# The first attention sequence of a 32-sequence transformer kernel in an order of its own

## The reference

```python
q = l2norm(q)
k = l2norm(k)
dots = jnp.einsum('bhid,bhjd->bhij', q, k) * QK_SCALE
dots = jnp.einsum('hg,bgij->bhij', W_pre_th, dots)
...
dots = jnp.where(causal[None, None], mask_value, dots)
top = jax.lax.top_k(dots, TOPK)[0]
vk = top[..., -1:]
dots = jnp.where(dots < vk, mask_value, dots)
attn = jax.nn.softmax(dots, axis=-1)
attn = jnp.einsum('hg,bgij->bhij', W_post_th, attn)
out = jnp.einsum('bhij,bhjd->bhid', attn, v)
...
out = out * jax.nn.sigmoid(gates)
return out @ Wo
```

## Time and profile before

| | us |
|---|---|
| three runs, median | 3628.78 |
| three runs, lowest and highest | 3628.4 and 3636.17 |
| the profiled execution | 3634.36 |
| its span, first to last instruction | 3633.1 |
| busy in the span: PE, DVE, ACT, POOL | 3390.1, 3437.1, 3092.9, 1745.4 |

### The profile page before, as it was taken

How to read it: one execution, slowest core, us unless ns; L and a number is a source line. 1 busy time by engine, 2 the same in 40 slices (tenths; PEclk the granted TensorE clock), 3 DMA queues, 4 the chain that set the end, 5 groups by cost and what they waited for, 6 DMA issues and landing times.

```text
span 3633.1 us, 78764 instructions
## 1 busy us (share of the span) xinstructions
PE 3390.1 (93%) x19287; PEld 2527.5 (70%) x19287; DVE 3437.1 (95%) x18664; ACT 3092.9 (85%) x10837; POOL 1745.4 (48%) x3670
## 2 busy tenths in 40 slices
PE   4999999986999999999999999999999999999987
PEld 2888888863666666676676666666666666666665
DVE  7999999936999999999999999999999999999993
ACT  6888888856898899989899898998998998898863
POOL 0000000014666666666666666666666666666663
PEclk9999999997999999999999999999999999999998
DMA  3000000002222222222222222222222222222210
GB/s 132 11 14 13 13 12 13 10 13 85 73 71 78 82 66 65 65 66 66 66 65 66 74 71 70 74 73 79 79 66 65 65 66 65 67 65 66 73 55 4
DMA packets 254141, 210.74 MB, mean 58 GB/s; under 512 B 78000, under 2 KB 234736, under 8 KB 252912
## 3 DMA queue, kind: packets, MB, share of 16 engines
q1 hardware_dynamic: 253680, 205.70, 18.1%
HBM read 93.97 MB, written 111.67 MB: 57 GB/s over the span
## 4 chain that ended last, share of the span: by engine, by line
PE 66%; ACT 17%; DVE 11%; issue 4%; POOL 2%; DMA 0%; SPq 0%; DVEq 0%; ACTq 0%; POOLq 0%
PE bank L378 10%; PE bank L221 8%; PE bank L1434 6%; PE bank L1422 5%; PE bank L1407 5%; PE bank L1465 3%; PE bank L469 3%; PE bank L195 3%; ACT SN L1618 3%; PE bank L1499 3%; DVE W L1826 3%; PE bank L1479 3%; PE bank L1438 3%; PE bank L346 3%; ACT sq L496 2%
## 5 line engine op out<-in xcount | busy, mean ns | idle before, releaser
L1826 DVE MATCH_REPLACE8 W<-last,W 128x130 f32<-128x130 f32 (+18 forms) x3456 | 871.9, 259 | 0.0
L1848 DVE MAX8 last<-W 128x8 f32<-128x130 f32 (+18 forms) x3456 | 762.9, 262 | 0.0
L1933 POOL TENSOR_SCALAR posts<-post,share 128x128 f32<-128x128 f32 x1024 | 366.7, 378 | 284.0 <-DVE share L1755 279.1
L1602 ACT ACTIVATE T<-T,peak 128x260 f32<-128x260 f32 (+15 forms) x1024 | 410.9, 409 | 3.5 <-POOL T L1984 2.4
L1618 ACT ACTIVATE SN<-bank,rq 128x260 f32<-128x260 f32 (+1 forms) x1024 | 357.9, 424 | 61.3 <-PE bank L1407 60.8
L1422 PE MATMUL bank<-T,pre 128*128 128x40 f32 (+15 forms) x1024 | 365.3, 439 | 14.4 <-ACT T L1626 10.1
L1434 PE MATMUL bank<-posts,T 128*128 128x128 f32 (+7 forms) x2048 | 311.7, 289 | 68.9 <-POOL posts L1933 60.6
L1984 POOL TENSOR_TENSOR T<-T,below 128x520 f32<-128x520 f32 (+12 forms) x416 | 360.3, 882 | 20.0 <-DVE below L1857 4.6
L1434 PEld LDWEIGHTS bank<-posts,T 128*128 128x128 f32 (+7 forms) x2048 | 249.0, 174 | 165.3 <-POOL posts L1933 88.9
L938 DVE TENSOR_TENSOR_SCAN hs<-dA,dx 128x256 f32<-128x256 f32 x512 | 349.9, 684 | 2.9 <-ACT dA L800 1.9
L1949 POOL TENSOR_TENSOR T<-T,w_mask 128x32 f32<-128x32 f32 x512 | 141.1, 278 | 412.6 <-ACT T L1626 410.2
(11 more groups left out here) (242 smaller groups left out, 9572.3 us busy)
## 6 DMA issues: line engine op xcount, KB each, us to landing
scores_by_token<-SN SPq DMA_DIRECT2D x64, 520.0 KB, 2.6
scores_by_token<-SN SPq DMA_DIRECT2D x64, 396.0 KB, 3.1
scores_by_token<-SN SPq DMA_DIRECT2D x32, 780.0 KB, 3.3
scores_by_token<-SN SPq DMA_DIRECT2D x32, 264.0 KB, 2.6
scores_by_token<-SN SPq DMA_DIRECT2D x32, 260.0 KB, 2.0
T<-scores_by_token SPq DMA_DIRECT2D x32, 244.0 KB, 3.0
T<-scores_by_token SPq DMA_DIRECT2D x32, 228.0 KB, 3.2
T<-scores_by_token SPq DMA_DIRECT2D x32, 212.0 KB, 3.8
```

The lines of the kernel that those rows point to most:

```text
L1602: act.activation(one, one, ACT.Exp, bias=peak[k % 2][:, j:j + 1], accum_out=total[k % 4][:, j:j + 1]).then_inc(e_made, 1)
L1826: dve.match_replace(both[:, s, at:to], best[n], both[:, s, at:to], LOWEST).then_inc(ranked, 1)
L1848: dve.max(best[n], both[:, s, at:to]).then_inc(ranked, 1)
L1933: pool.tensor_scalar(posts[(4 * k + j) % NP][:], post[:], share[k % 2][:, j:j + 1], 1.0, ALU.mult, ALU.mult).then_inc(posts_made, 1)
```

## The change

1. **The first sequence ahead of the tables.** For b = 0 the sixteen pieces of blk 1 are made first, then the six of blk 0, into a ring of six banks instead of three. Even pieces are copied by ACT (`first_keep`), odd ones by DVE (11 groups of `TENSOR_SCALAR`, semaphore `s_halved`). Blk 0's scores are kept in `T8[1]`, which is empty then. SP stages blk 1, then blk 0, and regroups pairs of blk 1 and blk 0 in turn (`FIRST`). All 16 premixes, copies and masks of b = 0 stand ahead of the first period, K pieces and squares of b = 1 before them, drops of quad 0 after the sixth mask. DVE clears `V2` and `T8[1]`, POOL no longer does. `tails()` comes in period 1 at beat 12, exponentials of quad 0 at beat 24, `q_clip` of b = 1 at beat 70.
2. **Narrow maxima ahead.** The maximum of quad i + 1's narrow pair (`largest`) stands inside quad i's wide steps, before the second halving; `top` has three buffers. Only quad 0's stays at the start.
3. **Marks by row.** The mark of row n waits for its own row's last `MAX8` only.
4. **Root sooner.** `PE_SPREAD2` 114 to 111, `POOL_ROOT2` 118 to 116.
5. **The last sequence** loads its exp table ahead of `nd.act_square`.

The diff, cut to its core:

```diff
+FIRST_SCORES = [(blk, piece) for blk in (1, 0) for piece in range(len(S_PIECES[blk]))]
...
+    FIRST = [(blk, k) for k in range(QUADS) for blk in (1, 0)]
...
-    top, last8 = room.sbs("top", [P, 4, 8], 2), room.sbs("last8", [P, 4, 8], 2)
+    top, last8 = room.sbs("top", [P, 4, 8], 3), room.sbs("last8", [P, 4, 8], 2)
...
+    FIRST_SN = (T8[1][:, 0:HEADS * W_LO].rearrange("p (h n) -> p h n", h=HEADS), SN)
+    FIRST_BANK = [*FRONT, *ATB, BACK[1]]
...
+    TAILS, FIRST_EXP, FIRST_CLIP = 12, 24, 70
...
-    PE_SPREAD2 = 114
+    PE_SPREAD2 = 111
...
-    POOL_ROOT2 = 118
+    POOL_ROOT2 = 116
...
             if seq(f):
...
+                else:
+                    stage(0, 1)
+                    stage(0, 0)
+                    for blk, k in FIRST:
+                        regroup(0, blk, (k,))
...
+        for blk, piece in FIRST_SCORES[::2]:
+            score(0, blk, piece)
+        for f in range(2):
+            front.k_piece(pe, 1, 0, f)
+        for blk, k in FIRST:
+            premix(0, blk, k)
...
+        first_keep()
+        for f in range(2):
+            front.k_square(act, 1, 0, f)
+        for blk, k in FIRST:
+            t_keep(0, blk, k)
+            if (blk, k) in ((0, 4), FIRST[-1]):
+                peaks(0, int(k > 4))
...
+                    if b == SEQS - 1:
+                        table(EXP_LN)
                     nd.act_square(act, b)
...
+        def largest(b, i):
...
+            dve.wait_ge(masked, masked_at(b, low))
+            dve.tensor_reduce(top[k % 3][:, 2:4, 0], side_by_side(b, low), AXIS.X, ALU.max).then_inc(ranked, 1)
...
                 if done == 3:
+                    if j0 == 0 and i + 1 < QUADS and QUAD[i + 1][2] not in WIDE:
+                        largest(b, i + 1)
+                        yield
...
-                dve.wait_ge(found_wide, 2 * ((QUADS + 1) * b + i + j0 // 2 + 1))
...
                 for n, (j, s) in enumerate(rows):
+                    dve.wait_ge(found_wide, 2 * ((QUADS + 1) * b + i + j0 // 2) + n + 1)
...
+        for n, (blk, piece) in enumerate(FIRST_SCORES):
+            if n % 2:
+                dve.wait_ge(s_made, n + 1)
...
+                    last = dve.tensor_scalar(FIRST_SN[blk][:, h, 0:w], FIRST_BANK[n % 6][:, j * w:(j + 1) * w], rq[:, c:c + 1], None, ALU.mult)
+                last.then_inc(s_halved, 1)
+        dve.memset(V2[:], 0.0)
+        for sent in staged[0]:
+            dve.wait_ge(sent, 16)
+        dve.memset(T8[1][:], 0.0).then_inc(blanked, 1)
...
+        for blk, k in FIRST:
+            hide(0, blk, k)
+            if (blk, k) == (0, 2):
+                turn_over(0, 0)
+                drop(0, 0)
+                front.k_clip(pool, 1, 0)
```

More of the change, by code:

```diff
@@ L1147, in attention_phase, with mixed_as, masked_at @@
     PREMIX = [list(range(HALF)), [g for i in range(QUADS) for g in (30 - 2 * i, 31 - 2 * i)]]
-    PAIR_AT = {g: (blk * HALF + k) // 2 for blk in range(2) for k, g in enumerate(PREMIX[blk])}
+    FIRST = [(blk, k) for k in range(QUADS) for blk in (1, 0)]
+    def mixed_as(b, blk, k):
+        return FIRST.index((blk, k)) if b == 0 else HALF * b + QUADS * blk + k
+    def masked_at(b, g):
+        blk = int(g >= HALF)
+        return mixed_as(b, blk, PREMIX[blk].index(g) // 2) + 1
     SN = room.sb("SN", [P, HEADS, KEYS])
@@ L1210, in rank_steps @@
     def rank_steps(i):
-        n = sum(17 for g in QUAD[i] if g in WIDE) + (QUAD[i][2] not in WIDE) + 2 * len(CUT[i])
+        n = sum(17 for g in QUAD[i] if g in WIDE) + (i == 0) + (i + 1 < QUADS and QUAD[i + 1][2] not in WIDE) + 2 * len(CUT[i])
         for g in QUAD[i]:
@@ L1327, in stage, with regroup @@
             for n, (lo, hi, pieces) in enumerate(STAGES[blk]):
-                sp.wait_ge(s_kept, S_ALL * b + S_BEFORE[blk] + pieces)
-                sp.dma_start(by_token[blk][:, lo:hi, 0:w], SN[:, lo:hi, 0:w]).then_inc(staged[blk][n], 16)
-        def regroup(b, blk):
+                if b:
+                    sp.wait_ge(s_kept, S_ALL * b + S_BEFORE[blk] + pieces)
+                else:
+                    kept = FIRST_SCORES.index((blk, 0)) + pieces
+                    sp.wait_ge(s_kept, kept)
+                    sp.wait_ge(s_halved, kept // 2)
+                by_head = SN if b else FIRST_SN[blk]
+                sp.dma_start(by_token[blk][:, lo:hi, 0:w], by_head[:, lo:hi, 0:w]).then_inc(staged[blk][n], 16)
+        def regroup(b, blk, pairs=range(HALF // 2)):
             if b == 1 and blk == 0:
-                sp.wait_ge(zeroed, 2)
+                sp.wait_ge(blanked, 1)
             if b >= 2 and blk == 0:
@@ L1338, in regroup @@
                 sp.wait_ge(sent, 16 * (b + 1))
-            for k in range(HALF // 2):
+            for k in pairs:
                 g = PREMIX[blk][2 * k]
@@ L1357, in sync @@
             if seq(f):
-                stage(f, 0)
-                regroup(f, 0)
-                stage(f, 1)
-                regroup(f, 1)
+                if f:
+                    for blk in range(2):
+                        stage(f, blk)
+                        regroup(f, blk)
+                else:
+                    stage(0, 1)
+                    stage(0, 0)
+                    for blk, k in FIRST:
+                        regroup(0, blk, (k,))
             if f == 0:
@@ L1393, in score @@
         def score(b, blk, piece):
-            n = S_BEFORE[blk] + piece
+            n = S_BEFORE[blk] + piece if b else FIRST_SCORES.index((blk, piece))
             if n == 0:
@@ L1406, in score @@
                     rows = slice(half * DH, (half + 1) * DH)
-                    last = pe.matmul(FRONT[(n + half) % 3][:, j * w:(j + 1) * w], qT[rows, even // 2, blk * P:(blk + 1) * P],
+                    last = pe.matmul((FRONT[(n + half) % 3] if b else FIRST_BANK[(n + half) % 6])[:, j * w:(j + 1) * w], qT[rows, even // 2, blk * P:(blk + 1) * P],
                                      kT[rows, even // 2, 0:w], start=True, stop=True)
@@ L1598, in exps @@
             else:
-                act.wait_ge(masked, HALF * b + PAIR_AT[QUAD[i][2 * pair]] + 1)
+                act.wait_ge(masked, masked_at(b, QUAD[i][2 * pair]))
             for j in (2 * pair, 2 * pair + 1):
@@ L1619, in s_keep, with first_keep @@
             last.then_inc(s_kept, 1)
+        def first_keep():
+            act.wait_ge(q_root.stepped, Root.STEPS)
+            for n, (blk, piece) in enumerate(FIRST_SCORES):
+                if n % 2 == 0:
+                    act.wait_ge(s_made, n + 1)
+                    w = (W_LO, W_HI)[blk]
+                    for j, h in enumerate(S_PIECES[blk][piece]):
+                        c = blk * HEADS + h
+                        last = act.activation(FIRST_SN[blk][:, h, 0:w], FIRST_BANK[n % 6][:, j * w:(j + 1) * w], ACT.Copy, scale=rq[:, c:c + 1])
+                    last.then_inc(s_kept, 2)
         def t_keep(b, blk, k):
             pair = pair_scores(b, PREMIX[blk][2 * k])
-            if (b, blk, k) == (0, 0, 0):
-                tails()
-            act.wait_ge(premixed, 2 * PAIRS * b + PAIRS * blk + k + 1)
+            act.wait_ge(premixed, mixed_as(b, blk, k) + 1)
             act.activation(pair, MIX[:, 0:pair.shape[-1]], ACT.Copy).then_inc(t_kept, 1)
@@ L1810, in wide @@
             rows = [(j, side(QUAD[i][j])) for j in (j0, j0 + 1)]
-            best = [top[k % 2][:, j, :] for j, _ in rows]
+            best = [top[k % 3][:, j, :] for j, _ in rows]
             for n, (j, s) in enumerate(rows):
@@ L1867, in rank @@
                 dve.wait_ge(peaked, k - 1)
-            if low not in WIDE:
-                dve.wait_ge(masked, HALF * b + PAIR_AT[low] + 1)
-                dve.tensor_reduce(top[k % 2][:, 2:4, 0], side_by_side(b, low), AXIS.X, ALU.max).then_inc(ranked, 1)
-                count += 1
+            if i == 0:
+                largest(b, i)
                 yield
```

77 lines of the change are left out of this document (47 added, 30 removed).

## The result

| | before | changed |
|---|---|---|
| median of 8 runs | 3628.35 us | 3642.37 us |
| lowest and highest | 3619.96 and 3636.17 | 3640.71 and 3643.46 |
| profiled execution, its span | 3634.36, 3633.1 | 3642.25, 3640.9 |
| ratio, 95% interval | | 1.0040 (1.0031 to 1.0048) |

The change costs 14 us. Forecast were 3620.5, faster, with a range of 3601 to 3632; the time lies above it.

What follows compares the result with a forecast made beforehand. The PE and ACT loop was taken as the bound, DVE nearly tied. From a median of 3628.8, −11.3 + 0.9 − 0.6 − 0.6 + 3.9 − 0.6 = −8.3 gave 3620.5 us, range 3601 to 3632.

Steps and rivals of the forecast that it cites:

- The start: Prologue: ranking of the first sequence starts at about 835.4 instead of 846.70, 11.3 us sooner (bounds 9 and 17).
- The fill on DVE: Prologue, DVE clearing T8[1]: 3.83 to 5.3 us, hidden behind transfers and first mix, 1.6 us of cover at worst.
- What comes back: First period: q_clip six beats later and PE's Q turn cost +1.5 us (0 to 2.6), net +0.9.
- Rival C: Prologue's gain swallowed: DVE memset, shared DMA queue or second sequence's premix late by 3 to 7 us; 3623.5 to 3627.5; chance 0.24.
- Maxima ahead and marks by row: Each period: 0.55 us less DVE work, only 0.02 on the path; −0.6 us in 30 periods, −0.6 in the last.
- Rival A: DVE is the bound: 17.6 us of DVE work and 6.6 of x_d waits come off; 3594, or 3601 without waits; chance 0.20.
- DVE's wait at the first halving: DVE at L1803 in each period: wait for POOL's mask grows from 0.36 to about 0.9 us.
- The waits for x_d: DVE's six waits on PE, 6.6 us in all, vanish with the root sooner, but gain nothing.
- Root sooner: PE's spread of nd's root, each period: a gap of 0.13 us (0 to 0.30), +3.9 us in all (0 to 9).
- rival B: Load of nd_rs after mix-back 4: spread waits longer, 30 us per us of gap, slower from 0.65 (3636 and more); chance 0.08.
- The table at the end: Last sequence: ACT's exp table load ahead of the squares no longer delays the root, −0.6 us.

Runs made afterwards that it cites:

- e7: Changed kernel with the root put back and the second sequence's whole K chain placed between the first sequence's sixteen mixes; 3619.88 us, 0.9980 of before.
- e11: Changed kernel, root put back, K steps among mixes from the fourth, tails ahead of mixes, quad 0-2 steps sooner, q_clip at beat 64; 3610.97 us, 0.9954 of before.
- e4: Kernel before with only the maxima ahead, marks by row and last table sooner (parts 2, 3, 5); 3623.41 us, 0.9996 of before.
- e2: Kernel before with only the nd root sooner (PE at beat 111, POOL at 116); 3631.15 us, 1.0013 of before.
- e12: Kernel before with root sooner, maxima ahead, marks by row and last table sooner, but the old first sequence; 3635.59 us, 1.0019 of before.
- e9: Kernel before with only the first sequence's new order (part 1), DVE's waits at the marks in their old order; 3639.30 us, 1.0027 of before.
- e3: Kernel before with only the first sequence's new order (part 1), one extra DVE wait per quad, mark waits exchanged; 3651.89 us, 1.0071 of before.
- e5: Kernel before with only the first sequence's new order (part 1), no extra quad wait, but DVE's two mark waits exchanged; 3656.50 us, 1.0076 of before.

## Why the prediction was wrong

**The start: right in its sum, with luck in its terms.** Forecast 835.4, measured 833.7. The scores with their copies took 8.3 us and not 13.5 (44 products at 810.33 and 6.13 us in the chain, then 2.19 of copies): back to back at the low clock four products took 0.86 us (810.90 to 811.76) and not the 1.24 of the single row that I had scaled, and the clock rose to its full level at about 813.5. The copies ended 6.5 us sooner than in my sum, but the last staging transfer landed 7.6 us behind them, at 826.26, and not 3.4. These two errors offset each other in good part. The fill on DVE took 3.79 us, inside my bounds of 3.83 and 5.3 but for 0.04, and ended 2.5 us ahead of the first maximum, which waited for POOL.

**What comes back: the step that failed.** I wrote that "q_clip for the second sequence moves from beat 64 to 70", priced the wait for quad 3's drops, gave 1.3 to "PE's own Q turn", and took +1.5. It was +19.6. I had treated the first period as one that shifts as a whole with its start. I followed the mixes in the order tables, and not what they were put ahead of: K's root, scaling and second product of the next sequence on three engines. In the trace of before that chain was in plain view (ACT at 846.23, half a microsecond ahead of the first ranking), and from q_clip to the second start are 48.0 us in before (884.44 to 932.46) and 50.0 in the changed kernel (889.13 to 939.09). Had I carried q_clip through the new order, the second start would have come out no sooner than before. e7 and e11 show the cause by moving it. I had also priced PE's clock for the scores alone: that the mixes would run at its low level, some 10 us on PE, stands in no term. Rival C named the outcome, and its sign came true (a start at 833.7 with a second start no sooner than before), but of its causes, the fill on DVE, the DMA queue and the premix of the second sequence, none was this chain, and its price of 3 to 7 us was too small.

**Maxima ahead and marks by row: right.** 0.5 us less of DVE work per period, of which next to nothing shows: e4 is at 0.9996. Rival A is out, and with it, for this kernel, the advice of the Trainium skill that sided with it ("Perfetto Trace Analysis", section "Identifying the Most-Contended Engine": optimise the engine with the highest occupancy first): DVE was 98.9% busy, and less work for it bought nothing that the times can tell. DVE's wait at the first halving grew by 0.24 us and not by 0.5; `share` now waits too, 31 times for 13.0 us in all. The waits for x_d went, as forecast.

**Root sooner: right mechanism, a third of its size.** The gap was forecast at 0.13, with 0.30 as its bound. Alone it is 0.09 by the period (e2). In the whole change it is 0.44 by the timeline and 0.5 by the period. I had kept POOL's times of before for a kernel whose DVE work I had moved. POOL's two marks together took 0.42 us longer, and its last drop and root came that much later against the mix-back. The decision point of rival B was 0.41 us of gap, and its sign, a period of 85.1 or more, came true. By its mechanism and place B was right, without the price of the first period that came on top. Its chance of 0.08 was too low: I had let no cost of one part depend on another part.

The Trainium skill has the rule that would have warned me ("SBUF — State Buffer", section "Who interferes with whom"): a DVE instruction with two inputs in SBUF contends with a GpSimd instruction that reads SBUF. The halvings have two such inputs, and the trace agrees in its direction: 706 ns against 842. Which of the two is held back depends, by the same page, on which was first. But the halvings ran beside these marks in the kernel before as well, for 463 ns of a mark on the mean and 537 in the changed one, so the overlap as such does not explain it; where in a mark it falls may. No run here moved the two against each other by hand, so that this is the cause of the 0.14 us is argued from the rows, not shown; that the gap needs the moved maxima and marks is shown (e2 against e12).

**The table at the end: right.** Forecast −0.6. PE's wait ahead of the last spread fell from 2.55 to 1.92 us (kernel before, then changed):

```profile
3629.52 1.22 PE L134 MATMUL bank<-w_ident,nd_rs 128*128 128x128 f32 x4 [2.55 <-POOL nd_rs L90]
```

```profile
3637.37 1.23 PE L135 MATMUL bank<-w_ident,nd_rs 128*128 128x128 f32 x4 [1.92 <-POOL nd_rs L91]
```

For the rest of the 4.2 us gained at the end the profiles show another clock. The granted clock was 0.53 and 0.50 in the kernel before while the last mix-back and the attention ran, and stayed full in the changed one. Whether the change has a part in that is open: from the last start to the end were 140.4 to 145.4 us in the kernels with parts 2 and 3, and 142.1 to 146.1 in those without. The windows, before and then changed (the clock is the third number from the end):

```profile
3580.00:3585.00 5.00, 3.47 (x14) 2.50 (x14) 0.00 (x0) 0.67 (x3) 1.86 (x5) 0.53 0.01 3
3585.00:3590.00 5.00, 4.05 (x30) 2.91 (x32) 0.00 (x0) 1.50 (x5) 0.11 (x1) 0.50 0.00 0
```

```profile
3592.00:3597.00 5.00, 2.97 (x29) 2.29 (x31) 0.00 (x0) 1.13 (x5) 1.42 (x4) 1.00 0.01 3
3597.00:3602.00 5.00, 5.00 (x78) 4.06 (x76) 0.00 (x0) 1.79 (x3) 3.02 (x3) 1.00 0.00 0
```

**The sum.** By the profile: −13.0 + 19.6 + 5.4 − 4.2 = +7.8 in span. The median moved by 14 since the profiled execution of before was 6 us above its own. The 30 periods grew by 5.4 and not by 30 × 0.48 = 14.4, as the profile of before has seven periods that are 0.9 us or more longer than the common one, and that of the changed kernel four. All profiles with parts 2 and 3 but without the early spread need 2544 to 2548 us for the 30 periods, those without these parts 2550 to 2555 (e2, e9, before; e3 and e5 with their later marks 2568), against which the timing of e4 shows no gain beyond its interval. Whether these parts make such long periods rarer stays open.

## What to carry to other kernels

When one item of a pipeline is pulled ahead of the tables, follow the *next* item's chain through every queue that the first one was pulled across. What matters is where the next start comes out, not where this one does. When two loops tie, as here, price the edits together: time taken off the tied engine bought next to nothing, time added cost nearly all of it, and an edit that empties a queue ahead of a wait should be costed with the durations that the other edits leave, not with those of before. Look at the clock of the stretch that an order leaves behind, too: a chain that alternates between PE and ACT ran here at half clock. To undo a part for an experiment, undo the order of its waits as well.

## What the runs showed that I had not expected

- **The order of two waits on one instruction.** With the wait that is long past first and the fresh one second, the mark came 0.11 us after the maximum that it needs; in the old order 0.04. Four pairs of marks per period, and as DVE tied with PE, together with what followed it made 17 us of 3639 (e5 at +0.76%, e9 at +0.27%).
- **The fill on DVE** of 4480 elements took 3.79 us, about what POOL needed (3.83), and less than the estimate of 4.67 that the prediction had worked out from the Trainium skill ("VectorE: DVE Perf Modes", section "Zero memsets can be issued as uint32 (trn2)"). The measurement decides.
- **POOL's marks stretched when DVE's work was moved**, by 0.14 us on the mean of the 128x116 marks (706 to 842 ns), though the marks themselves were the same work as before. Parts 2, 3 and 5 alone bring it to 796 ns (e4_rank_and_table), the root alone leaves it at 698 (e2_root_alone).
- **The clock of a chain that alternates.** Through the sixteen mixes of the first sequence, from 829 to 859 us, PE was granted 0.50 throughout; with the K steps among them it was 0.74 from 840 to 860 us (e11_k_order2).
